# One stack of 128 quotient rows, a residual added by TensorE and copied out by ScalarE: the tail of a one-core graph attention kernel

## The chip, the cores and the metric

The kernel runs on one core of a Trainium2 chip. The metric is the device time of one execution in microseconds (us), median over runs; lower is better.

## The reference

Inputs: `x` (512 targets x 128), `adj` (512 x 512, zeros and ones, sparse), `h_neigh` (512 neighbours x 128), weights `Wq`, `Wk`, `Wv`, `Wo` (128 x 128) with biases, edge embeddings `E` (2 x 128). There are 8 heads of 16 dimensions.

```python
h = jnp.maximum(_layernorm(x, axis=-1), 0.0)
msg = h_neigh[None, :, :] + E[edge_types]          # edge_types is adj
q = (h_target @ Wq.T + bq).reshape(Bt, H, DH)      # h_target is h
k = (msg @ Wk.T + bk).reshape(Bt, Bn, H, DH)
v = (msg @ Wv.T + bv).reshape(Bt, Bn, H, DH)
scores = jnp.einsum('bhd,bnhd->bhn', q, k) / np.sqrt(DH)
scores = jnp.where(adjacency[:, None, :] == 0, -1e9, scores)
attn = jax.nn.softmax(scores, axis=-1)             # masked entries set to 0 after it
out = jnp.einsum('bhn,bnhd->bhd', attn, v).reshape(Bt, d)
return x + (out @ Wo.T + bo)
```

## The kernel before, in words

Every engine has a program of its own, written out by hand; semaphores tie them together. Each engine runs its own instructions strictly in the written order, and the order of the score tiles is the list `ORDER` (32 tiles, one per head `h` and block `t` of 128 neighbours; heads 6 and 7 are interleaved at the end, so that places 24 to 31 are the tiles of these two heads and place 31 is head 7, block 3).

**Start.** SyncE loads `x`, then the pack `pw` (the transposed `Wq` and `Wv`, and two 128x128 forms of `Wo`, 256 KB in all), then bias rows; ScalarE's queue loads `h_neigh` with `Wk`, then the adjacency in both layouts (1 MB each). VectorE computes the layer norm, TensorE turns it and projects q, k and v. For exactness q and k are split in three bf16 parts, gathered per head into `stack`. GpSimd adds `bo` to `x` early on (`resid`, line 238).

**Middle.** For each head, TensorE scores by target (lines 563 and 577), VectorE finds the masked row maximum (line 426), GpSimd splits the maximum in two bf16 parts (lines 225, 227), TensorE turns it (line 586) and ScalarE places it in the head's stack (line 323). Then TensorE scores by neighbour with the maximum already taken off (line 609), and ScalarE takes the exponential (line 351). What is not an edge is removed in one of three ways, by tile: GpSimd multiplies the exponentials by zero or one (`ON_POOL`, line 233); VectorE subtracts a veto of 2^30 from the scores on their way to the exponential (`ON_DVE`, line 446, here place 18 and places 21 to 30); or TensorE adds minus the veto in a product ahead of the scores (`ON_PE`, line 604: the rest, place 31 among them).

**Products with V.** Exponentials times `V` give 16 numerators and one denominator for each head; four heads (a "group") lie in the four 32-row quarters of a bank. Group 0 (heads 0 to 3) is accumulated in bank 5 (line 623). Group 1 (heads 4 to 7) is accumulated in two pieces, `PIECES = ((0, 3), (3, 1))`: target blocks 0 to 2 (384 columns, bank 0) and target block 3 (128 columns, bank 3), line 633.

**Tail.** `normalise(step, bank, g, first, tiles)` on VectorE (line 462) turns the 32x32 blocks of a bank (line 467), takes the reciprocal of the denominators (469), multiplies (471) and turns the quotients back into `ctxT` (476). It runs for group 0 (512 columns), for piece 0 of group 1 and for piece 1 of group 1. In `turned_U` each head keeps 32 columns of which 16 carry data, so a group fills the 128 rows of `ctxT` half, and `Wo` comes in two forms with zero rows in between, one for each group. `project_out(i, g)` on TensorE (line 639) multiplies by that form: 4 products for group 0, then 3 for piece 0 and 1 for piece 1 of group 1, accumulated in banks 4 and 5. `finish(i)` on VectorE (line 485) adds `resid` and writes `y`, SyncE stores piece 0 (192 KB, line 189) and ScalarE's queue stores piece 1 (64 KB, line 356). VectorE's order at the end is: maskings of places 21 to 30, `normalise` of group 0, of piece 0, of piece 1, `finish(0)`, `finish(1)`. Nothing follows the exponential of place 31 on ScalarE but the issue of the last store.

Of the kernel before, what the change touches and what calls it, by code (L numbers as in the profile page):

```python
# [5 lines left out]
B, N, D, H = 512, 512, 128, 8  # L6
DH = D // H
P = 128
BT, NT = B // P, N // P
# [9 lines left out]
G = 2  # L19
HG = H // G  # L20
CT = P // HG
# [13 lines left out]
PIECES = ((0, 3), (3, BT - 3))  # L35
# [3 lines left out]
TAIL_ACC, TAIL_OUT = (0, 3), (4, 5)  # L39
# [3 lines left out]
ORDER = [(h, t) for h in range(H - 2) for t in range(NT)] + [(h, t) for t in range(NT) for h in (H - 2, H - 1)]  # L43
# [2 lines left out]

LIVE_TILES = (1, 3)
ON_POOL = [(1, 1), (2, 1), (2, 3), (0, 1), (1, 3), (3, 1), (0, 3), (3, 3), (4, 1), (4, 3)]
ON_DVE = [ORDER[18]] + ORDER[21:31]
ON_PE = [tile for tile in ORDER if tile not in ON_POOL and tile not in ON_DVE]  # L50

A_BEFORE = (9, 9, 10, 12, 14, 15, 16, 17, 18, 18, 20, 21, 22, 23, 24, 26, 27, 28, 28, 30)
# [12 lines left out]
def gnn_kernel(nc, x_in, adj_b, adj_n, pack_k, pack_w, bias_rows, out):  # L65
    f32, bf16, i32 = mybir.dt.float32, mybir.dt.bfloat16, mybir.dt.int32
    ACT = mybir.ActivationFunctionType
    ALU = mybir.AluOpType
# [3 lines left out]
    with ctx:  # L72
        def sb(name, shape, dt=f32):
            return ctx.enter_context(nc.sbuf_tensor(name, shape, dt))

        def sem(name):
# [12 lines left out]
        pk = sb("pk", [P, N + D + 4])  # L89
        hnT, wkT = pk[:, 0:N], pk[:, N:N + D]  # L90
        bq_col, bk_col, e1_col = (pk[:, N + D + i:N + D + i + 1] for i in range(3))
        pw = sb("pw", [P, 4 * D])
        wqT, wvT = pw[:, 0:D], pw[:, D:2 * D]
        brow = sb("brow", [P, 2 * D])
        bv_row, bo_row = brow[:, 0:D], brow[:, D:2 * D]
        msgT = sb("msgT", [P, N])
# [11 lines left out]
        masked_scores = sb("masked_scores", [P, len(A_BANKS), N], bf16)  # L108
        masked_n = sb("masked_n", [P, len(ON_DVE), B])
        row_max = sb("row_max", [P, H, BT])  # L110
        max_parts = sb("max_parts", [P, H, MAX_ROWS, BT], bf16)
        prob = sb("prob", [P, H, NT, B])
        ident = sb("ident", [P, P])
# [8 lines left out]
        turned_U = sb("turned_U", [P, G, B // CT, CT])  # L122

        tiny_row = sb("tiny_row", [1, P], bf16)
        recip = sb("recip", [P, G, B // CT])
        ctxT = sb("ctxT", [P, G, B])
        resid = sb("resid", [P, BT, D])
        y = sb("y", [P, BT, D])
        ps = ctx.enter_context(nc.psum_tensor("ps", [P, 8, 512], f32))
# [34 lines left out]
        u_turned, recip_ready, u_scaled, ctx_ready = (  # L164
            sem("u_turned"), sem("recip_ready"), sem("u_scaled"), sem("ctx_ready"))
        tiny_zero, tiny_set = sem("tiny_zero"), sem("tiny_set")
        out_projected, resid_ready, y_ready = sem("out_projected"), sem("resid_ready"), sem("y_ready")
# [106 lines left out]
        def _(act):  # L274
# [69 lines left out]
            for k, (h, t) in enumerate(ORDER):  # L344
                if (h, t) in ON_DVE:
                    act.wait_ge(masked_ready, count_upto(ON_DVE, (h, t)))
                    scores = masked_n[:, ON_DVE.index((h, t)), :]
                else:
                    act.wait_ge(scores_n, k + 1)
                    scores = ps[:, B_BANKS[k % len(B_BANKS)], :]  # L350
                nc.scalar.activation(prob[:, h, t, :], scores, ACT.Exp, scale=DH ** -0.5).then_inc(exp_done, 1)  # L351
                for head, placed_at in PLACED_AT.items():
                    if placed_at == k:
                        place_max(head)
            act.wait_ge(y_ready, 2)
            act.dma_start(out[:, PIECES[1][0] * D:BT * D], y[:, PIECES[1][0]:BT, :]).then_inc(stored[1], 16)
            act.wait_ge(stored[1], 16)
# [2 lines left out]
        def _(dve):  # L360
# [6 lines left out]
            for t in range(BT):  # L367
                last = nc.vector.bn_stats(stats[:, t, :], xt[:, t, :])  # L368
            last.then_inc(stats_ready, 1)
            dve.wait_ge(stats_ready, 1)  # L370
            for t in range(BT):
                last = nc.vector.bn_aggr(mean_var[:, t, :], stats[:, t, :])
# [89 lines left out]
            def normalise(step, bank, g, first, tiles):  # L462

                blocks = slice(first * P // CT, (first + tiles) * P // CT)
                at = slice(first * P, (first + tiles) * P)
                dve.wait_ge(pv_done, step + 1)
                nc.vector.transpose(turned_U[:, g, blocks, :], ps[:, bank, 0:tiles * P]).then_inc(u_turned, 1)  # L467
                dve.wait_ge(u_turned, step + 1)
                nc.vector.reciprocal(recip[:, g, blocks], turned_U[:, g, blocks, DH]).then_inc(recip_ready, 1)
                dve.wait_ge(recip_ready, step + 1)  # L470
                nc.vector.tensor_tensor(
                    turned_U[:, g, blocks, 0:DH], turned_U[:, g, blocks, 0:DH],
                    recip[:, g, blocks].rearrange("p (k c) -> p k c", c=1).to_broadcast([P, tiles * P // CT, DH]),
                    ALU.mult).then_inc(u_scaled, 1)
                dve.wait_ge(u_scaled, step + 1)
                nc.vector.transpose(ctxT[:, g, at], turned_U[:, g, blocks, :].rearrange("p k c -> p (k c)")).then_inc(  # L476
                    ctx_ready, 1)

            dve.wait_ge(veto_last_ready, 1)
            dve.wait_ge(veto_odd_ready, 1)  # L480
# [1 line left out]
                mask_scores(*tile)  # L482
            normalise(0, ACC_BANK, 0, 0, BT)

            def finish(i):
                tiles = slice(PIECES[i][0], sum(PIECES[i]))
                dve.wait_ge(resid_ready, 1)
                dve.wait_ge(out_projected, 1 + i)
                nc.vector.tensor_tensor(y[:, tiles, :],  # L489
                                        ps[:, TAIL_OUT[i], :].rearrange("p (t c) -> p t c", t=BT)[:, tiles, :],  # L490
                                        resid[:, tiles, :], ALU.add).then_inc(y_ready, 1)

            normalise(1, TAIL_ACC[0], 1, *PIECES[0])
            normalise(2, TAIL_ACC[1], 1, *PIECES[1])
            finish(0)
            finish(1)

        @block.tensor
        def _(pe):

            pe.wait_ge(ones_set, 1)
            for _ in range(WARM_UP):
# [4 lines left out]
                             skip_group_check=True).then_inc(k_projected, 1)  # L507
            pe.wait_ge(idents_ready, 3)
            for i in range(HALVES):
                for t in range(HT * i, HT * (i + 1)):  # L510
                    pe.wait_ge(xn_ready, t + 1)
                    last = nc.tensor.transpose(ps[:, HT_BANKS[i], (t % HT) * P:(t % HT + 1) * P], xn[:, t, :],  # L512
                                               ident[:, :])
# [31 lines left out]
            for i in range(HALVES):  # L545
                pe.wait_ge(hT_ready[i], 1)
                nc.tensor.matmul(ps[:, Q_BANKS[i], 0:HB], wqT, hT[:, i * HB:(i + 1) * HB], start=True, stop=False,  # L547
                                 skip_group_check=True).then_inc(q_projected[i], 1)
# [87 lines left out]
                if t == V_LAST[i][-1]:  # L636
                    last.then_inc(pv_done, 1)

            def project_out(i, g):

                pe.wait_ge(ctx_ready, 1 if g == 0 else 2 + i)
                first, tiles = PIECES[i]
                for t in range(first, first + tiles):
                    last = nc.tensor.matmul(ps[:, TAIL_OUT[i], t * D:(t + 1) * D], ctxT[:, g, t * P:(t + 1) * P],  # L644
                                            pw[:, (2 + g) * D:(3 + g) * D], start=g == 0 and t == first, stop=g == G - 1,
                                            skip_group_check=True)
                if g == G - 1:
                    last.then_inc(out_projected, 1)

            for i in range(HALVES):  # L650
                pe.wait_ge(q_part_ready[i], PARTS)
# [38 lines left out]
                last_product_with_v(0, t)  # L690
            for t in V_LAST[1]:
                last_product_with_v(1, t)
            project_out(0, 0)
            project_out(1, 0)
            project_out(0, 1)
            project_out(1, 1)


# [34 lines left out]
```

## Time and profile before

| what | us |
|---|---|
| median of 3 runs | 52.49 (52.41 to 52.53) |
| the profiled execution, its own time | 52.74 |
| its span, first to last instruction | 50.6 |
| TensorE products / VectorE / ScalarE / GpSimd busy | 44.1 / 40.3 / 34.7 / 31.0 |
| mean granted clock of TensorE | 0.99 |

The times of single instructions in the rows below are in microseconds from the start of the span. The profiled execution spent 52.74 - 50.6 = 2.14 us outside its span. PE is TensorE (PEld its weight loads), DVE VectorE, ACT ScalarE, POOL GpSimd, SP SyncE.

### The profile page before, as it was taken

To read this page: it belongs to the slowest core of one execution; us is meant where nothing else is said; L and a number is where in the kernel's file an instruction comes from. 1 tells how busy PE (TensorE), PEld (TensorE's weight loads), DVE (VectorE), ACT (ScalarE), POOL (GpSimd) and SP (SyncE) were. 2 spreads that over 40 slices of the span, in tenths; PEclk is the share of its full clock that TensorE was granted. 3 is DMA by queue.
4 is the path that set the end of the run, shared out by engine and by line. 5 is a ranking of instruction groups with operands and counts; after the bars stand their busy time and mean duration, and the time that the engine had idled before them with its cause. 6 is when DMAs were issued, how large, how long until landed. Compare 5 with 4: busy or idle time off the path is not lost.

```text
span 50.6 us, 844 instructions
## 1 busy us (share of the span) xinstructions
PE 44.1 (87%) x257; PEld 17.8 (35%) x260; DVE 40.3 (80%) x115; ACT 34.7 (68%) x60; POOL 31.0 (61%) x50
## 2 busy tenths in 40 slices
PE   0899879978999679899999999999999998999800
PEld 0333215824445233234344424142222023288500
DVE  2011879598489999799999999799997999989820
ACT  0380657789996978979999898897199999400000
POOL 5790001999999999547599959990999930000000
PEclk9999999999999999999999999999999999999996
DMA  0689999960099999700000000000000000000032
GB/s 0 76 219 431 435 379 235 403 269 2 10 212 193 184 295 201 154 2 0 0 0 0 0 6 0 13 0 0 0 0 0 0 0 0 13 0 0 0 118 89
DMA packets 2070, 4.98 MB, mean 98 GB/s; under 512 B 258, under 2 KB 658, under 8 KB 1810
## 3 DMA queue, kind: packets, MB, share of 16 engines
q1 hardware_dynamic: 1490, 2.44, 21.2%
q10 hardware_dynamic: 576, 2.49, 12.7%
q8 instruction: 2, 0.03, 0.3%
q14 instruction: 2, 0.02, 0.1%
HBM read 3.08 MB, written 0.26 MB: 66 GB/s over the span
## 4 chain that ended last, share of the span: by engine, by line
PE 62%; DVE 15%; DMA 8%; ACT 5%; issue 3%; DVEq 0%
PE ps L609 15%; PE ps L577 11%; DMA xt<-x_dram 8%; PE ps L623 8%; PE ps L563 7%; PE ps L633 6%; PE ps L586 4%; PE ps L604 3%; PE ps L547 2%; PE ps L512 2%; DVE ctxT L476 2%; DVE stats L368 2%; DVE split L396 2%; DVE y L489 2%; DVE turned_U L467 2%
## 5 line engine op out<-in xcount | busy, mean ns | idle before, releaser
L426 DVE CUSTOM_DVE_ANT_0 masked_scores<-ps,mask_b 128x512 bf16<-128x512 f32 x32 | 20.1, 687 | 1.7 <-PE ps L563 1.0
L233 POOL TENSOR_TENSOR prob<-prob,live 128x512 int32<-128x512 int32 x10 | 12.6, 1275 | 0.0
L351 ACT ACTIVATE prob<-ps 128x512 f32<-128x512 f32 x21 | 11.4, 598 | 1.1 <-PE ps L609 0.8
L609 PE MATMUL ps<-stack 98*128 98x512 bf16 x32 | 10.9, 381 | 0.6 <-ACT stack L323 0.4
L577 PE MATMUL ps<-stack 96*128 96x512 bf16 x28 | 9.6, 384 | 0.2
L215 POOL TENSOR_SCALAR mask_b<-adj_b_sb 128x512 bf16<-128x512 int32 x3 | 6.3, 2111 | 4.8 <-DMA adj_b_sb<-adj_b_dram 4.8
L351 ACT ACTIVATE prob<-masked_n 128x512 f32<-128x512 f32 x11 | 6.4, 626 | 1.5 <-DVE masked_n L446 1.4
L446 DVE TENSOR_TENSOR masked_n<-ps,veto 128x512 f32<-128x512 f32 x11 | 6.8, 683 | 0.4 <-PE ps L609 0.3
L503 PE MATMUL ps<-ones 128*128 128x512 bf16 x10 | 4.2, 604 | 1.4 <-DVE ones L361 1.4
L323 ACT ACTIVATE stack<-ps 2x512 bf16<-2x512 f32 x8 | 4.7, 590 | 0.4
L609 PEld LDWEIGHTS ps<-stack 98*128 98x128 bf16 x32 | 2.8, 97 | 6.0 <-DVE masked_n L446 2.2
L623 PE MATMUL ps<-prob,V 128*32 128x512 f32 x32 | 4.3, 605 | 0.0
L577 PEld LDWEIGHTS ps<-stack 96*128 96x128 bf16 x28 | 2.5, 96 | 4.9 <-DVE row_max L426 2.7
L220 POOL TENSOR_SCALAR live<-adj_n_sb 128x512 int32<-128x512 int32 x2 | 4.1, 2048 | 0.0
L633 PE MATMUL ps<-prob,V 128*32 128x384 f32 (+1 forms) x64 | 4.0, 384 | 0.0
L225 POOL CAST max_parts<-row_max 128x4 bf16<-128x4 f32 x8 | 1.6, 203 | 3.6 <-DVE row_max L426 3.6
L563 PE MATMUL ps<-k_head,q 128*128 128x512 f32 x8 | 3.7, 605 | 0.0
L586 PE MATMUL ps<-minus,max_parts 128*2 128x128 bf16 x32 | 3.1, 218 | 0.4 <-POOL max_parts L227 0.4
L604 PE MATMUL ps<-veto,minus 128*128 128x512 bf16 x8 | 3.0, 380 | 0.0
L279 ACT ACT_TABLE_LOAD x1 | 1.3, 1283 | 2.1 <-issue 2.1
L586 PEld LDWEIGHTS ps<-minus,max_parts 128*2 128x2 bf16 x32 | 1.6, 82 | 3.3 <-POOL max_parts L227 2.7
L644 PE MATMUL ps<-pw,ctxT 128*128 128x128 f32 x16 | 2.6, 294 | 0.1
(71 smaller groups left out, 54.8 us busy)
## 6 DMA issues: line engine op xcount, KB each, us to landing
stack<-split SPq DMA_DIRECT2D x8, 192.0 KB, 4.0
adj_b_sb<-adj_b_dram ACTq DMA_DIRECT2D x1, 1024.0 KB, 7.4
adj_n_sb<-adj_n_dram ACTq DMA_DIRECT2D x1, 1024.0 KB, 10.1
pk<-pack_k_dram ACTq DMA_DIRECT2D x1, 322.0 KB, 4.4
xt<-x_dram SPq DMA_DIRECT2D x1, 256.0 KB, 4.2
pw<-pack_w_dram SPq DMA_DIRECT2D x1, 256.0 KB, 6.0
out_dram<-y SPq DMA_DIRECT2D x1, 192.0 KB, 2.0
brow<-bias_rows_dram SPq DMA_DIRECT2D x1, 128.0 KB, 9.1
```

Source lines behind the costliest of these rows:

```text
L215: nc.gpsimd.tensor_scalar(mask_b[:, t, :], adj_b_sb[:, t * N:(t + 1) * N], 0.0, MASKED, ALU.is_equal, ALU.mult).then_inc(mask_b_pool_ready, 1)
L233: nc.gpsimd.tensor_tensor(bits, bits, live[:, LIVE_TILES.index(t), :], ALU.mult).then_inc(cut_done, 1)
L323: nc.scalar.activation(stack[PAIR_ROWS:STACK, h, SIDE["q"], :], ps[PAIR_ROWS:STACK, MAX_BANK, :], ACT.Copy).then_inc(max_placed, 1)
L351: nc.scalar.activation(prob[:, h, t, :], scores, ACT.Exp, scale=DH ** -0.5).then_inc(exp_done, 1)
L426: nc.vector.tensor_tensor_reduce(out=masked_scores[:, k % len(A_BANKS), :], in0=ps[:, A_BANKS[k % len(A_BANKS)], :], in1=mask_b[:, t, :], ...
L446: nc.vector.tensor_tensor(masked_n[:, ON_DVE.index((h, t)), :], ps[:, B_BANKS[k % len(B_BANKS)], :], veto[:, t, :], ALU.subtract).then_inc ...
L563: nc.tensor.matmul(ps[:, bank, :], q32[:, t * P:(t + 1) * P], k_head_0[:, :], start=True, stop=True).then_inc(scores_b, 1)
L577: nc.tensor.matmul(ps[:, A_BANKS[k % len(A_BANKS)], :], stack[0:PAIR_ROWS, h, SIDE["q"], t * P:(t + 1) * P], stack[0:PAIR_ROWS, h, SIDE["k ...
L586: last = nc.tensor.matmul(ps[PAIR_ROWS:STACK, MAX_BANK, t * P:(t + 1) * P], max_parts[:, h, :, t], minus16[:, :], start=True, stop=True)
L609: nc.tensor.matmul(bank, stack[0:STACK, h, SIDE["k"], t * P:(t + 1) * P], stack[0:STACK, h, SIDE["q"], :], start=(h, t) not in ON_PE, stop ...
L623: last = nc.tensor.matmul(ps[j * CT:(j + 1) * CT, ACC_BANK, :], V[:, t, j, :], prob[:, j, t, :], start=False, stop=t == V_FIRST[-1], tile_ ...
L633: last = nc.tensor.matmul(ps[j * CT:(j + 1) * CT, TAIL_ACC[i], 0:tiles * P], V[:, t, HG + j, :], prob[:, HG + j, t, first * P:(first + til ...
```

## The change

1. The last tile of the order, place 31, is masked by VectorE in place of TensorE: `ON_DVE` takes one tile more, and its veto product (line 604) goes.
2. The multiplication by the reciprocals writes group 0's 16 columns of each 32-column block beside group 1's in a new tile `scaled`. One turn back for each piece (`turn_back`) gives the rows of both groups, 128 full rows, and `Wo` comes in one form: 4 products in place of 8, and `pw` has 192 KB. Group 0's own turn back goes.
3. TensorE adds `resid` with two products by the identity (`add_resid`, 384 and 128 columns, fp32), after VectorE has read bank 5.
4. ScalarE copies the two finished pieces to `y`, after its last exponential, and VectorE's two additions go.

```diff
-ON_DVE = [ORDER[18]] + ORDER[21:31]
+ON_DVE = [ORDER[18]] + ORDER[21:32]
...
-        pw = sb("pw", [P, 4 * D])
+        pw = sb("pw", [P, 3 * D])
...
+        scaled = sb("scaled", [P, B // CT, CT])
+        ctxT = sb("ctxT", [P, B])
...
+            def finish(i):
+                tiles = slice(PIECES[i][0], sum(PIECES[i]))
+                act.wait_ge(out_projected, 1 + i)
+                nc.scalar.activation(y[:, tiles, :], ps[:, TAIL_OUT[i], :].rearrange("p (t c) -> p t c", t=BT)[:, tiles, :],
+                                     ACT.Copy).then_inc(y_ready, 1)
+
+            for i in range(len(PIECES)):
+                finish(i)
             act.wait_ge(y_ready, 2)
...
                 nc.vector.tensor_tensor(
-                    turned_U[:, g, blocks, 0:DH], turned_U[:, g, blocks, 0:DH],
+                    scaled[:, blocks, g * DH:(g + 1) * DH], turned_U[:, g, blocks, 0:DH],
...
-                dve.wait_ge(u_scaled, step + 1)
-                nc.vector.transpose(ctxT[:, g, at], turned_U[:, g, blocks, :].rearrange("p k c -> p (k c)")).then_inc(
-                    ctx_ready, 1)
+            def turn_back(i):
+                first, tiles = PIECES[i]
+                dve.wait_ge(u_scaled, 2 + i)
+                nc.vector.transpose(ctxT[:, first * P:(first + tiles) * P],
+                                    scaled[:, first * P // CT:(first + tiles) * P // CT, :].rearrange(
+                                        "p k c -> p (k c)")).then_inc(ctx_ready, 1)
...
-            normalise(1, TAIL_ACC[0], 1, *PIECES[0])
-            normalise(2, TAIL_ACC[1], 1, *PIECES[1])
-            finish(0)
-            finish(1)
+            for i in range(len(PIECES)):
+                normalise(1 + i, TAIL_ACC[i], 1, *PIECES[i])
+                turn_back(i)
...
+            def add_resid(i):
+                first, tiles = PIECES[i]
+                pe.wait_ge(resid_ready, 1)
+                nc.tensor.matmul(ps[:, TAIL_OUT[i], first * D:(first + tiles) * D], ident[:, :],
+                                 resid[:, first:first + tiles, :].rearrange("p t c -> p (t c)"), start=True, stop=False,
+                                 skip_group_check=True)
+
+            def project_out(i):
+                first, tiles = PIECES[i]
+                pe.wait_ge(ctx_ready, 1 + i)
                 for t in range(first, first + tiles):
-                    last = nc.tensor.matmul(ps[:, TAIL_OUT[i], t * D:(t + 1) * D], ctxT[:, g, t * P:(t + 1) * P],
-                                            pw[:, (2 + g) * D:(3 + g) * D], start=g == 0 and t == first, stop=g == G - 1,
-                                            skip_group_check=True)
+                    last = nc.tensor.matmul(ps[:, TAIL_OUT[i], t * D:(t + 1) * D], ctxT[:, t * P:(t + 1) * P], woT,
+                                            start=False, stop=t == first + tiles - 1, skip_group_check=True)
...
-            project_out(0, 0)
-            project_out(1, 0)
-            project_out(0, 1)
-            project_out(1, 1)
+            pe.wait_ge(u_turned, 1)
+            for i in range(len(PIECES)):
+                add_resid(i)
+            for i in range(len(PIECES)):
+                project_out(i)
```

## Rows read from the trace of the kernel before

**Rows 1.** The end of the chain that ended last: start, us, what.

```profile
42.28 2.26 PE ps L633 x24
44.57 0.59 DVE turned_U L467
...
47.13 0.31 DVE ctxT L476
...
47.52 0.53 DVE y L489
...
48.09 0.29 DVE y L489
```

**Rows 2.** Timeline of VectorE: start, us, engine, line, op, tiles, count [idle before].

```profile
38.63 3.68 DVE L446 TENSOR_TENSOR masked_n<-ps,veto 128x512 f32<-128x512 f32 x6 [0.30 <-PE ps L609]
42.23 0.70 DVE L467 STREAM_TRANSPOSE turned_U<-ps 128x512 f32<-128x512 f32 x1
...
43.72 0.71 DVE L476 STREAM_TRANSPOSE ctxT<-turned_U 128x512 f32<-128x512 f32 x1
...
45.84 0.58 DVE L476 STREAM_TRANSPOSE ctxT<-turned_U 128x384 f32<-128x384 f32 x1
```

**Rows 3.** Timeline of ScalarE, the last two exponentials.

```profile
42.34 0.63 ACT L351 ACTIVATE prob<-masked_n 128x512 f32<-128x512 f32 x1
...
43.00 0.60 ACT L351 ACTIVATE prob<-ps 128x512 f32<-128x512 f32 x1
```

**Rows 4.** Timeline of TensorE and its weight loads, from place 31 on.

```profile
41.90 0.38 PE L609 MATMUL ps<-stack 98*128 98x512 bf16 x1 [0.16 <-DVE masked_n L446]
...
43.65 0.16 PEld L633 LDWEIGHTS ps<-prob,V 128*32 128x32 f32 x8 [0.63 <-ACT prob L351]
...
45.30 0.97 PEld L644 LDWEIGHTS ps<-pw,ctxT 128*128 128x128 f32 x8 [0.20 <-issue]
...
46.47 0.74 PEld L644 LDWEIGHTS ps<-pw,ctxT 128*128 128x128 f32 x6 [0.20 <-DVE ctxT L476]
...
46.91 0.50 PE L644 MATMUL ps<-pw,ctxT 128*128 128x128 f32 x3
...
47.49 0.49 PE L644 MATMUL ps<-pw,ctxT 128*128 128x128 f32 x2
```

**Rows 5.** Groups by shape: line, engine, op, tiles, count | busy us, mean ns.

```profile
L563 PE MATMUL ps<-k_head,q 128*128 128x512 f32 x8 | 3.7, 605 | 0.0
...
L633 PE MATMUL ps<-prob,V 128*32 128x384 f32 x32 | 3.1, 495 | 0.0
...
L336 ACT ACTIVATE V<-ps 128x512 f32<-128x512 f32 x1 | 0.6, 597 | 0.5 <-PE ps L534 0.5
...
L304 ACT ACTIVATE hT<-ps 128x256 f32<-128x256 f32 x2 | 0.8, 384 | 0.3
...
L318 ACT ACTIVATE warm<-eps 128x1 f32<-128x1 f32 x1 | 0.2, 203 | 0.0
```

**Rows 6.** One piece of that chain in its middle, a veto product.

```profile
19.63 0.22 PE ps L604
```

**Rows 7.** The two stores: their issue, then KB and us to landing.

```profile
48.10 0.35 SPq L189 DMA_DIRECT2D out_dram<-y  x1
48.41 0.35 ACTq L356 DMA_DIRECT2D out_dram<-y  x1
...
out_dram<-y SPq DMA_DIRECT2D x1, 192.0 KB, 2.0
out_dram<-y ACTq DMA_DIRECT2D x1, 64.0 KB, 1.8
```

**Rows 8.** The stores' transfer by stretches: A:B, us, TensorE's granted clock, DMA share, GB/s.

```profile
49.15:49.40 0.25, 1.00 1.05 393
```

**Rows 9.** The loads: TensorE's wait at the q projection, the load of pw.

```profile
8.38 0.30 PEld L547 LDWEIGHTS ps<-hT,pw 128*128 128x128 f32 x2 [0.21 <-issue]
...
pw<-pack_w_dram SPq DMA_DIRECT2D x1, 256.0 KB, 6.0
```

More of the change, by code:

```diff
@@ L91, in gnn_kernel @@
         bq_col, bk_col, e1_col = (pk[:, N + D + i:N + D + i + 1] for i in range(3))
-        pw = sb("pw", [P, 4 * D])
-        wqT, wvT = pw[:, 0:D], pw[:, D:2 * D]
+        pw = sb("pw", [P, 3 * D])
+        wqT, wvT, woT = pw[:, 0:D], pw[:, D:2 * D], pw[:, 2 * D:3 * D]
         brow = sb("brow", [P, 2 * D])
@@ L125, in gnn_kernel @@
         recip = sb("recip", [P, G, B // CT])
-        ctxT = sb("ctxT", [P, G, B])
+        scaled = sb("scaled", [P, B // CT, CT])
+        ctxT = sb("ctxT", [P, B])
         resid = sb("resid", [P, BT, D])
@@ L464, in normalise @@
                 blocks = slice(first * P // CT, (first + tiles) * P // CT)
-                at = slice(first * P, (first + tiles) * P)
                 dve.wait_ge(pv_done, step + 1)
@@ L483, in _ @@
             normalise(0, ACC_BANK, 0, 0, BT)
[L485 to L491, printed above, removed]
-            normalise(1, TAIL_ACC[0], 1, *PIECES[0])
-            normalise(2, TAIL_ACC[1], 1, *PIECES[1])
-            finish(0)
-            finish(1)
+            for i in range(len(PIECES)):
+                normalise(1 + i, TAIL_ACC[i], 1, *PIECES[i])
+                turn_back(i)
         @block.tensor
@@ L637, in last_product_with_v @@
                     last.then_inc(pv_done, 1)
-            def project_out(i, g):
-                pe.wait_ge(ctx_ready, 1 if g == 0 else 2 + i)
+            def add_resid(i):
                 first, tiles = PIECES[i]
-                for t in range(first, first + tiles):
-                    last = nc.tensor.matmul(ps[:, TAIL_OUT[i], t * D:(t + 1) * D], ctxT[:, g, t * P:(t + 1) * P],
-                                            pw[:, (2 + g) * D:(3 + g) * D], start=g == 0 and t == first, stop=g == G - 1,
-                                            skip_group_check=True)
-                if g == G - 1:
-                    last.then_inc(out_projected, 1)
+                pe.wait_ge(resid_ready, 1)
[5 more added lines that the diff above has]
+                pe.wait_ge(ctx_ready, 1 + i)
+                for t in range(first, first + tiles):
+                    last = nc.tensor.matmul(ps[:, TAIL_OUT[i], t * D:(t + 1) * D], ctxT[:, t * P:(t + 1) * P], woT,
+                                            start=False, stop=t == first + tiles - 1, skip_group_check=True)
+                last.then_inc(out_projected, 1)
             for i in range(HALVES):
@@ L712, in by_dim @@
         return w.reshape(H, DH, -1).transpose(1, 0, 2).reshape(D, -1)
-    wo = np.zeros((G, HG, CT, D), Wo.dtype)
-    wo[:, :, :DH] = Wo.T.reshape(G, HG, DH, D)
+    wo = Wo.T.reshape(G, HG, DH, D).transpose(1, 0, 2, 3).reshape(P, D)
     cols = [by_dim(bq), by_dim(bk), E[1][:, None], np.zeros((D, 1), E.dtype)]
@@ L722 @@
         "pack_k_dram": np.concatenate([hn.T, by_dim(Wk).T, *cols], axis=1),
-        "pack_w_dram": np.concatenate([by_dim(Wq).T, Wv.T, *wo.reshape(G, P, D)], axis=1),
+        "pack_w_dram": np.concatenate([by_dim(Wq).T, Wv.T, wo], axis=1),
         "bias_rows_dram": np.concatenate([bv, bo])[None],
```

## The prediction, made before the changed kernel ran

> **What bounds the kernel now.** I read the chain that ended last first, from its end backwards, because everything the change touches lies in the last 9 us. It ends in VectorE: turn, reciprocal, product and turn back of piece 0, the same four for piece 1 until 47.44, then the addition of piece 0 and, right behind it on the same engine, that of piece 1, over at 48.38 [rows 1]. Only then is the second store issued, at 48.41, and it lands 1.8 us later, at 50.2; the first, issued at 48.10, lands at 50.1 [rows 7]. Ahead of 44.57 the chain names TensorE's products with V [rows 1]. The timelines correct that: the last eight of piece 0 had their weights loaded at 43.65, after a wait of 0.63 us for ScalarE [rows 4], whose exponential of place 31 ran from 43.00 to 43.60 [rows 3]. It could not start before, since the exponential of place 30 ended at 42.97, and that one had started at 42.34 behind VectorE's masking of place 30: six maskings in 3.68 us, 0.68 each, so started 0.60 apart, the last from 41.63 to 42.31 [rows 2]. So the path to the end is: masking of place 30 on VectorE, two exponentials, products with V, VectorE's eight steps, two additions, the store.
>
> **The veto of place 31.** Its product on TensorE goes, worth 0.22 us there [rows 6], so the scores that began at 41.90 and took 0.38 [rows 4] begin at about 41.68 and are there at 42.06. VectorE's new masking is next after place 30's. By the spacing it starts at 42.23 (where the turn of group 0 starts now) and ends at 42.91; the scores are there 0.17 us before. The exponential follows a masking by 0.03 us (42.31 to 42.34 [rows 2, 3]): 42.94, and as one that reads `masked_n` it takes 0.63 in place of 0.60, until 43.57 against 43.60. Gain 0.03. The bounds: if the masking starts only when place 30's has ended (42.34), the exponential runs from 43.05 to 43.68, a loss of 0.08; better than 0.03 it can hardly be, as the masking is bound by the one before. I take 0.03, the spacing of the five pairs in [rows 2]. TensorE's own 0.22 is worth nothing: it waits for ScalarE at 43.65 anyway.
>
> **Group 0's steps on VectorE** start 0.60 later, at 42.83. They lose the turn back of 0.71 us; what is left took from 42.23 to 43.72 (1.49 us) [rows 2] and now ends at 44.32. Piece 0's first turn can start at 44.54, so 0.22 us cover it. The removed turn back ended at 44.43 before 44.57, and so was hidden: no gain from it. If VectorE were late by more than that, each further part would come straight off the end.
>
> **VectorE's eight steps for group 1** keep their shapes (the turn back of piece 0 has 128x384 before and after, 0.58 us [rows 2]); only the target of the product moves. I cost this at nothing. Their last ends at 47.44 - 0.03 = 47.41.
>
> **TensorE between 45.27 and the first turn back.** Before, group 0's four products (8 instructions, loads for 0.97 us from 45.30 [rows 4]) filled this gap, and piece 0's weights were loaded at 46.47, behind the turn back that ended at 46.42. Now two products by the identity stand there, 512 fp32 columns in all. Head 0's eight instructions of 512 columns were busy for 3.7 us together [rows 5] and make up four products of that width, so 512 columns cost 0.93 us: done at 46.20. The first turn back is there at 46.39: cover 0.19. The lower bound of the effect is nothing. The upper bound takes durations without overlap, 2 x 0.495 for 384 columns [rows 5] and 0.49 for the pair of 128 [rows 4], 1.48 us: done at 46.75, late by 0.36. I take the first, since it is the same kind of product, back to back on the same engine. The new wait for VectorE's turn of group 0 (over at 42.83 + 0.70 = 43.53) holds up nothing at 45.27, and `resid` was made long before.
>
> **Three products, then one.** The work behind each turn back is the same: piece 0's ends at 47.41 now [rows 4], 47.38 then; piece 1's load starts 0.05 after the turn back, 47.46, and the product takes 0.49 [rows 4]: 47.95.
>
> **The additions go, ScalarE's copies come.** ScalarE has been idle since 43.60, and behind its two new waits for TensorE only the second store's issue is queued; SyncE waits for copy 0 as it did for the addition. Copies from the accumulation banks took 0.597 us for 512 columns and 0.384 for 256 [rows 5]; straight between and beyond, 384 columns take 0.49 and 128 take 0.28. Copy 0: 47.41 to 47.90, SyncE's store issued at 47.92 against 48.10. Copy 1 waits for TensorE (47.95 + 0.03 = 47.98) and no longer for the engine: 47.98 to 48.26, the store issued at 48.29 against 48.41. Before, 47.44 to the last y took 0.94 us; now it takes 0.85. Bounds: as long as the next larger shape (0.597 and 0.384), copy 1 runs from 48.04 to 48.42, a loss of 0.04 at the issue; as short as the nearest smaller (0.384 and 0.203), a gain of 0.20. I take the straight line, since two points of the same engine give it.
>
> The rule table of the Trainium skill's page "ScalarE: Activation LUTs" (Rules for kernel authors) says to give `add` and its like to VectorE, up to about three times faster per element in bf16. Here, fp32 from the banks, VectorE's own last steps took 0.53 and 0.29 us [rows 1], no less than the line for ScalarE gives. By the page's formula for an ACTIVATE (186 ns + 0.833 ns per column) an estimate for the copies is 0.506 and 0.293 us, and the sum would be 0.015 us longer.
>
> **The loads.** `pw` shrinks from 256 to 192 KB. It is the second load on SyncE's queue and landed 6.0 us after its issue, and TensorE's q projection at 8.38 waited for no transfer [rows 9]. No gain; 64 KB less traffic beside the adjacency could only help steps that don't bind. If a load did come later by a few hundredths, it would show there.
>
> **Sum.** Second store issued 0.03 + 0.09 = 0.12 us earlier; the profiled execution would have taken 52.74 - 0.12 = 52.62. That execution was 0.25 above the median of the runs shown, so I put the same difference on the median: 52.49 - 0.12 = 52.37. A measurement of this kernel can tell about 0.2% (0.1 us) from no change, so this forecast lies just beyond that.
>
> **Rivals.**
> *A, the stores share their way (chance 0.10).* In 49.15 to 49.40 the 16 DMA engines were fully busy with both stores [rows 8]. If the bytes' end is set by when the bulk begins, the first store counts, which is issued 0.18 earlier: 52.31. Against it: the second store is the last to land, and its issue moved only 0.12. The Trainium skill's page "Trainium Kernel Development and Optimization" (Key Constraints) says that transfers from the SP and ACT queues run on the same 16 engines and interleave; by that rule the first one's start counts too, and the sum would be this rival's.
> *B, the gain is eaten (0.23).* If the masking of place 31 starts at 42.34, the tail is 0.08 late and the copies give 0.09 back: 52.48. If ScalarE's copies are as long as the larger shapes, the store is issued 0.04 later than before: 52.53. For it: 0.03 us decide in the hand-over between two engines. Against: the five equal spacings.
> *C, slower: the identity products come too late (0.10).* They stand on TensorE right in front of the products that the first turn back releases. The point from which it decides is 46.39. Done at 46.75, they put the end of piece 0's products at 47.74 and piece 1's right behind, so that ScalarE's copies follow each other: 47.77 to 48.26 and 48.29 to 48.57. The store is issued at 48.60, 0.19 later than before: 52.68. For it: fp32, 512 columns, and nothing left out. Against: the measured spacing.
> *D, the change does not free what it says (0.05).* If VectorE, with one masking more, is not ready at 44.54 (group 0's steps longer than the 1.71 us from 42.83), piece 0 starts late by the rest; with 0.2 us over, 52.57.
>
> **The numbers.** Forecast 0.52, A 0.10, B 0.23, C 0.10, D 0.05. The forecast's and A's spread lies around the bound of 0.1 us: I count 0.47 of their 0.62 as faster by over 0.2%. Within 0.2%: their other 0.15, 0.20 of B and 0.03 of D, together 0.38. Slower: C with 0.10 and the far ends of B (0.03) and D (0.02), 0.15. The range goes from 52.25 (A with copies at their short bound) to 52.60, which leaves C out.
>
> **What would show it.** The exponential of place 31 reads `masked_n`, starts near 42.94 and is over by 43.60. VectorE is idle for about 0.2 us before the turn of piece 0 (44.54). TensorE's loads of the identity end by 46.2, with a wait for the turn back at 46.4 behind them. ScalarE shows copies of 0.49 and 0.28 us, the second waiting for TensorE; the stores are issued near 47.9 and 48.3. I am wrong if TensorE is still adding the residual when the turn back ends, if the chain goes through both copies, or if the last store is issued earlier and the end does not move.

## The result, and the profile after

The changed kernel takes 52.09 us, median of 20 runs (51.74 to 52.68), against 52.53 us for the kernel before (20 runs beside it, 52.04 to 52.98). The ratio is 0.9925, 95% interval 0.9902 to 0.9948. The ratios here leave out the executions that took over 1.5% longer than the fastest of the same kernel (three of these 20), while medians and mean spans take in all. The forecast was 52.37 with a range from 52.25 to 52.60: the right sign, but the gain is 0.44 us where 0.12 was forecast.

The profiled execution of the changed kernel took 51.80 us with a span of 49.8 us. Its chain that ended last, from the last group of maskings on (start, us, what):

```profile
35.18 0.70 DVE masked_n L458
...
37.18 5.74 ACT prob L354 x10
42.91 0.04 issue
42.96 0.90 PE ps L640 x8
43.85 0.02 issue
43.88 0.59 DVE turned_U L478
...
45.15 0.58 DVE ctxT L491
...
46.44 0.32 DVE ctxT L491
46.76 0.04 issue
46.80 0.50 PE ps L658 x2
47.30 0.02 issue
47.33 0.28 ACT y L362
```

Beside [rows 1]: the two additions at the end of VectorE are gone; behind the last turn back (46.75) there is TensorE's one product and ScalarE's short copy. Every step also begins some 0.7 us earlier than it did, long before the code that was changed. The timelines of VectorE, ScalarE, TensorE with its loads, and the issues of the stores:

```profile
35.18 2.48 DVE L458 TENSOR_TENSOR masked_n<-ps,veto 128x512 f32<-128x512 f32 x4
37.96 4.28 DVE L458 TENSOR_TENSOR masked_n<-ps,veto 128x512 f32<-128x512 f32 x7 [0.30 <-PE ps L616]
42.16 0.71 DVE L478 STREAM_TRANSPOSE turned_U<-ps 128x512 f32<-128x512 f32 x1
...
43.88 0.58 DVE L478 STREAM_TRANSPOSE turned_U<-ps 128x384 f32<-128x384 f32 x1 [0.27 <-PE ps L640]
...
37.18 5.73 ACT L354 ACTIVATE prob<-masked_n 128x512 f32<-128x512 f32 x10
46.76 0.84 ACT L362 ACTIVATE y<-ps 128x384 f32<-128x384 f32 x2 [3.85 <-PE ps L658]
47.63 0.35 ACTq L368 DMA_DIRECT2D out_dram<-y  x1
...
44.61 1.13 PE L650 MATMUL ps<-resid,ident 128*128 128x384 f32 x4
...
45.78 0.74 PEld L658 LDWEIGHTS ps<-pw,ctxT 128*128 128x128 f32 x6 [0.23 <-DVE ctxT L491]
...
47.27 0.35 SPq L192 DMA_DIRECT2D out_dram<-y  x1
```

What to see. Seven maskings in 4.28 us keep the spacing of 0.60 (six in 3.68 [rows 2]). VectorE is idle for 0.27 us before the turn of piece 0. The identity products lie between 44.61 and 45.74, and the load for piece 0's projection follows the turn back (45.73) by 0.05, as before (46.42 to 46.47 [rows 4]).

ScalarE's copies by shape (line, engine, op, tiles, count | busy us, mean ns | idle before) have the forecast's lengths:

```profile
L362 ACT ACTIVATE y<-ps 128x384 f32<-128x384 f32 x1 | 0.5, 491 | 3.9 <-PE ps L658 3.9
...
L362 ACT ACTIVATE y<-ps 128x128 f32<-128x128 f32 x1 | 0.3, 278 | 0.1
```

To take the start out of the comparison I measure from the start of the last four maskings in a row (`masked_n` x4; 35.85 before, 35.18 here) to the issue of the second store (48.41 [rows 7], 47.63 here): 12.56 us before, 12.45 in the changed kernel. In all later traces with the same tail this stretch came out within 0.01 us of the same value, while its start lay anywhere from 35.18 to 36.03 us (without the runs that hold a load back). So a tail's price can be read from one trace, and a start's only from many executions. To the issue of the first store the stretch is 12.25 us before and 12.09 after; that this one counts too is shown further down.

### The profile page after: what moved, and what is told of

It is laid out like the page before. It is cut to its first block and busy times, and to the rows that moved or that the text cites. A ratio compares the mean times of both kernels' runs of the same rounds, so it can differ in the third digit from the quotient of the medians.

```text
span 49.8 us, 833 instructions
## 1 busy us (share of the span) xinstructions
PE 44.0 (88%) x253; PEld 17.7 (35%) x255; DVE 39.4 (79%) x113; ACT 35.3 (71%) x62; POOL 30.7 (62%) x50
## 3 DMA queue, kind: packets, MB, share of 16 engines
q10 hardware_dynamic: 576, 2.49, 13.1%
## 5 line engine op out<-in xcount | busy, mean ns | idle before, releaser
L354 ACT ACTIVATE prob<-ps 128x512 f32<-128x512 f32 x20 | 10.8, 598 | 1.0 <-PE ps L616 0.8
L354 ACT ACTIVATE prob<-masked_n 128x512 f32<-128x512 f32 x12 | 7.0, 628 | 1.5 <-DVE masked_n L458 1.4
L458 DVE TENSOR_TENSOR masked_n<-ps,veto 128x512 f32<-128x512 f32 x12 | 7.4, 683 | 0.4 <-PE ps L616 0.3
L362 ACT ACTIVATE y<-ps 128x384 f32<-128x384 f32 (+1 forms) x2 | 0.8, 384 | 3.9 <-PE ps L658 3.9
```

Source lines behind the costliest of these rows:

```text
L458: nc.vector.tensor_tensor(masked_n[:, ON_DVE.index((h, t)), :], ps[:, B_BANKS[k % len(B_BANKS)], :], veto[:, t, :], ALU.subtract).then_inc ...
```

## The experiments

Theory T: the whole gain lies in the tail. Theory L: the part over 0.12 us comes from the loads, because `pw` has 64 KB less. Theory N: the start only varies by chance. All times are set against runs of the kernel before on the same chip.

**1. The changed kernel again** (no edit).

> The changed kernel once more, on the chip of this set, as the measure for the others. Both theories: a ratio near 0.9925, some 0.4 us faster than the kernel before. Of that my sum gives the tail 0.12 us; theory L (loads) gives the other 0.27 us to the load of x, which lands earlier because pw has 64 KB less; theory T (tail) has all of it behind 42 us.

Measured: 52.04 us against 52.57, ratio 0.9882 (0.9842 to 0.9922, 6 runs). The tail's stretch is 12.45, the time from the second store's issue to the end of the span 2.15 (2.23 and 2.20 in two traces of the kernel before), and outside the span 2.02 (2.10).

The end follows the first store's issue more closely than the second's. In all twenty traces it comes 2.49 to 2.54 us after the first. After the second it comes 2.19 to 2.23 us later where the two are issued 0.30 or 0.31 apart (eleven traces), and 2.14 to 2.16 where they are 0.36 or 0.37 apart (nine).

**2. The changed kernel with `pw` at 256 KB.**

```diff
-        pw = sb("pw", [P, 3 * D])
+        pw = sb("pw", [P, 4 * D])
...
-np.concatenate([by_dim(Wq).T, Wv.T, wo], axis=1)
+np.concatenate([by_dim(Wq).T, Wv.T, wo, np.zeros((P, D), Wo.dtype)], axis=1)
```

> The changed kernel with pw padded to 256 KB again (64 KB of zeros nobody reads). Theory L: about 0.27 us of the gain goes, ratio near 0.998, and x lands about 0.3 us later than in the changed kernel (median over executions; a single trace can differ by as much). Theory T: ratio stays at 0.9925. Theory N (x's landing varies between executions and has nothing to do with pw): ratio stays too.

Measured: 52.32 us, ratio 0.9945 (0.9912 to 0.9977). That is nearer to T's and N's 0.9925 than to L's 0.998, but the changed kernel beside it had 0.9882, and against that the gain shrinks, which neither T nor N explains. But x had landed 3.8 us after its issue in its trace, no later than in run 1. What that trace shows late is another thing, the k projection. TensorE's rows of run 2 (two loads of the warm-up, the k projection, x's turn; then its stretch from 6 to 7 us with busy time, granted clock 1.00, DMA share and GB/s), and then those of run 1:

```profile
3.98 0.15 PEld L510 LDWEIGHTS ps<-ones 128*128 128x128 bf16 x1 [0.28 <-issue]
4.41 0.15 PEld L510 LDWEIGHTS ps<-ones 128*128 128x128 bf16 x1 [0.28 <-issue]
...
5.68 1.85 PE L513 MATMUL ps<-msgT,pk 128*128 128x512 f32 x2
...
7.37 0.66 PE L519 MATMUL ps<-ident,xn 128*128 128x128 f32 x4
...
6.00:7.00 1.00, 1.00 (x2) 1.00 1.06 428
```

```profile
5.51 1.12 PE L513 MATMUL ps<-msgT,pk 128*128 128x512 f32 x2 [0.33 <-ACT msgT L285]
6.95 1.00 PE L519 MATMUL ps<-ident,xn 128*128 128x128 f32 x4 [0.32 <-DVE xn L391]
...
6.00:7.00 1.00, 0.68 (x3) 1.00 1.04 397
```

The same two instructions took 1.85 us in one execution and 1.12 in the other. The warm-up products ahead of them were started 0.43 us apart for 512 bf16 columns, which is the 1.2 GHz level; the 512 bf16 columns of a veto product later took 0.22 [rows 6], 2.4 GHz. In run 2 the k projection still ran at the lower level, in run 1 at the upper one. The view's granted clock reads 1.00 in the stretch from 6 to 7 us in both, because it counts the time ahead of the trace's first clock record as 1.00. That first record is the rise to 2.4 GHz itself: 7.30 us after the start of the span in run 2, 4.32 in run 1. Over the twenty traces it lies between 4.13 and 7.35 us.

**3. The kernel before with `pw` at 192 KB and the last 64 KB later.**

```diff
-            sp.dma_start(pw[:, :], pack_w).then_inc(pw_loaded, 16)
+            sp.dma_start(pw[:, 0:3 * D], pack_w).then_inc(pw_loaded, 16)
...
+            sp.wait_ge(x_loaded, 16)
+            sp.dma_start(pw[:, 3 * D:4 * D], pack_wo).then_inc(wo_loaded, 16)
...
+            pe.wait_ge(wo_loaded, 16)
             project_out(0, 0)
```

> The kernel before, with pw loaded as 192 KB at its place and the last 64 KB (group 1's form of Wo) in a load of its own on SyncE's queue once x is in. Theory L: ratio near 0.995 (0.27 us faster) with the tail unchanged. Theories T and N: 1.000.

Measured: 52.28 us, ratio 0.9932 (0.9900 to 0.9964), with the tail's stretch at 12.56 as before. T falls as the whole explanation: a version without any of the tail's changes gains 0.27 us. But this trace too spent 2.02 us outside the span, not 2.10, so part of it is no matter of loads. (The last line of the edit, one wait more on TensorE, is also in runs 5, 6 and 10, which load a part of `pw` by itself.)

**4. The changed kernel with place 31's veto on TensorE.**

```diff
-ON_DVE = [ORDER[18]] + ORDER[21:32]
+ON_DVE = [ORDER[18]] + ORDER[21:31]
```

> The changed kernel with place 31's veto back on TensorE. By my sum the exponential of place 31 ends 0.03 us later: ratio 0.9925 + 0.0006, not to be told apart in the time, but the trace shows it starting 0.66 us after that of place 30 rather than 0.60. If the masking on VectorE costs or gives more than that, the time moves by over 0.1 us.

Measured: 52.18 us, ratio 0.9912 (0.9875 to 0.9949), not to be told from the changed kernel. The stretch is 12.47 against 12.45, and the exponential of place 31 starts 0.66 us after that of place 30, as expected: part 1 is worth 0.02 us where the prediction had 0.03.

**5 to 7. Smaller and larger `pw`.** Run 5 is the kernel before with 128 KB in `pw` and both forms of Wo later; run 6 the changed kernel with Wo later; run 7 the changed kernel with `pw` padded to 512 KB.

```diff
+            sp.dma_start(pw[:, 0:2 * D], pack_w).then_inc(pw_loaded, 16)
...
+            sp.wait_ge(x_loaded, 16)
+            sp.dma_start(pw[:, 2 * D:4 * D], pack_wo).then_inc(wo_loaded, 16)
```

(In run 6 the later load is `pw[:, 2 * D:3 * D]`; in run 7 the edit is that of run 2 with five blocks of zeros.)

> The kernel before with pw cut to 128 KB (Wq and Wv) and both forms of Wo (128 KB) loaded later, on SyncE's queue once x is in; the tail as before. Theory L (bytes issued early beside x and the k pack cost time): twice the step of the 192 KB run, 0.3 to 0.55 us faster than before, ratio 0.990 to 0.994. Theory N (spread of executions): 1.000 within 0.003.

> The changed kernel with Wo (64 KB) taken out of pw and loaded later in the same way. Theory L: another 0.1 to 0.3 us faster than the changed kernel, ratio 0.985 to 0.990. Theory N: as the changed kernel, 0.991 to 0.9925.

> The changed kernel with pw padded to 512 KB by zeros nobody reads (320 KB more, still early enough for TensorE's q projection if the engines keep 430 GB/s). Theory L with a price per byte (0.3 us for 64 KB): over 1 us slower than the changed kernel. Theory L with a price by sharing of the 16 engines (64 KB at 430 GB/s is 0.15 us): 0.4 to 0.75 us slower than the changed kernel. Theory N: as the changed kernel.

Measured: run 5 52.29 us, ratio 0.9956 (0.9929 to 0.9983); run 6 52.12, 0.9937 (0.9895 to 0.9979); run 7 52.31, 0.9958 (0.9925 to 0.9991). Neither form of L's price holds: 128 KB bring no more than 192, and 512 KB cost no more than 256. N's 1.000 within 0.003 for run 5 is met only if the share outside the span, 0.08 us or 0.0015, is taken off. What remains of L is a step between 192 and 256 KB.

**8. VectorE copies in place of ScalarE.**

```diff
+            def finish(i):
+                tiles = slice(PIECES[i][0], sum(PIECES[i]))
+                dve.wait_ge(out_projected, 1 + i)
+                nc.vector.tensor_copy(y[:, tiles, :],
+                                      ps[:, TAIL_OUT[i], :].rearrange("p (t c) -> p t c", t=BT)[:, tiles, :]
+                                      ).then_inc(y_ready, 1)
```

(behind both `turn_back`s on VectorE; ScalarE's `finish` is left out.)

> The changed kernel with VectorE in place of ScalarE copying the two pieces out. One look, read from the start of the last maskings (the first VectorE masking of the group of four) to the issue of the second store, which was 12.56 us before and 12.45 us in the changed kernel. A copy by VectorE of 384 columns from the banks starts when TensorE's three products end (about as now) and takes 0.53 to 0.56 us: the second copy takes 0.29, so 12.46 to 12.50 if VectorE is as good, since it is free by then. So nearly all of the tail's gain is the order of work (first piece finished before the second product ends), not the engine; theory S (ScalarE's shorter copy carries the gain): 12.56.

Its timeline at the end:

```profile
47.18 0.86 DVE L500 COPY y<-ps 128x384 f32<-128x384 f32 x2
47.22 0.30 PEld L660 LDWEIGHTS ps<-pw,ctxT 128*128 128x128 f32 x2 [0.27 <-DVE ctxT L483]
47.77 0.36 SPq L192 DMA_DIRECT2D out_dram<-y  x1
48.07 0.35 ACTq L360 DMA_DIRECT2D out_dram<-y  x1
```

The stretch is 12.47, where ScalarE's copies give 12.45: theory S falls, ScalarE itself is worth 0.02 at the issue of the second store. At the end of the span it is worth more: from the start of the same maskings to the end run 8 takes 14.66 us, the nine traces with ScalarE's copies 14.58 to 14.62, the kernel before 14.77 to 14.79. The first copy is the longer one by 0.07 on VectorE (0.558 against 0.491), so the first store is issued 12.17 us into the stretch in place of 12.09. Of the tail's 0.11 us at the second store's issue, 0.02 come from place 31 (run 4) and 0.02 from ScalarE, so 0.07 are left for what run 8 has in common with the changed kernel. They lie in front of the first copy: before, the addition began at 47.52, 0.08 behind the last turn back (47.44, [rows 1]); VectorE's copy began at 47.18, 0.01 behind it (46.86 + 0.31). The addition waited for two semaphores, `resid_ready` and `out_projected`, the copy for one; that this makes the 0.07 is argued, not tested.

**9, 17, 18. `pw` held back until x is in** (kernel before, one line).

```diff
+            sp.wait_ge(x_loaded, 16)
             sp.dma_start(pw[:, :], pack_w).then_inc(pw_loaded, 16)
```

> The kernel before, with the issue of pw (256 KB, unchanged) held on SyncE until x has landed; the bias rows and ones queue behind it. Theory L-share (pw's rows delay x's on the shared DMA engines): x lands well before the 3.7 to 4.2 us after its issue seen so far, 3.2 to 3.6; the time falls by 0.2 us or more unless pw itself then comes too late for the q projection (pw would land near 8, needed at 7.9 to 8.4), in which case the trace shows TensorE waiting for pw. Theory N (x's landing is not pw's doing): x lands at 3.7 to 4.2 as before, and the time rises by pw's lateness or stays.

> The kernel before with pw held until x has landed, second look. If pw's bytes beside x's are what delays x: first use of x at 4.35 to 4.55 us. If not: 4.6 to 5.0 as in the traces with pw at 256 KB.

> The same kernel, third look; the same expectation: 4.35 to 4.55 us if pw beside x is the cause, 4.6 to 5.0 if not.

Measured in run 9: 55.89 us, median of six (54.51 to 58.36); the ratio 1.0422 (1.0328 to 1.0516) is that of the two shortest alone. Runs 17 and 18 are one execution each, 55.40 and 55.73 us. `pw` comes too late, as TensorE's load at the q projection shows in run 9.

```profile
4.69 0.88 DVE L369 BATCH_NORM_STATS2 stats<-xt 128x6 f32<-128x128 f32 x4 [1.83 <-DMA xt<-x_dram]
...
10.58 1.35 PEld L548 LDWEIGHTS ps<-hT,pw 128*128 128x128 f32 x4 [2.26 <-DMA pw<-pack_w_dram]
```

For x it is the first row that counts. With nothing of `pw` in flight, x's first use began at 4.69, 4.55 and 4.61 us in the three traces. It did not come earlier than with `pw` at 192 KB beside it (4.34 to 4.66), and x landed 3.8 to 3.9 us after its issue, not 3.2 to 3.6. Three traces are few against the spread, but they give no support to plain sharing of the DMA engines between `pw` and x.

**10. The same 256 KB as two loads with rows of 1 KB** (kernel before).

```diff
-            sp.dma_start(pw[:, :], pack_w).then_inc(pw_loaded, 16)
+            sp.dma_start(pw[:, 0:2 * D], pack_w).then_inc(pw_loaded, 16)
+            sp.dma_start(pw[:, 2 * D:4 * D], pack_wo).then_inc(wo_loaded, 16)
```

> The kernel before, with pw's 256 KB issued at the same place as two loads of 128 KB (rows of 1 KB each in place of rows of 2 KB). Theory L-rows (what counts is the size of pw's rows next to x's last rows; 1 and 1.5 KB are alike, 2 and 4 KB are alike in the runs so far): about 0.25 us faster than before, ratio 0.995. Theory L-bytes (what counts is the bytes queued right behind x): 1.000 within 0.002. Theory N: 1.000.

Measured: 52.27 us, ratio 0.9961 (0.9924 to 0.9997). That is 0.2 us, of which 0.08 lie outside the span (2.02 again). The mean span is 50.32 us (+-0.15) against 50.45 (+-0.04): too close to tell rows from bytes. With the 0.08 us taken off, theory N's 1.000 is within the interval too.

**11. The kernel before again** (no edit).

> The kernel before once more, one look, for where x lands and how long the k projection takes. Theory L: x lands 3.9 us or more after its issue. Theory N: anywhere from 3.6 to 4.2. The stretch from the start of the last four maskings to the second store's issue is 12.56 us whatever the start.

Measured: 52.31 us (one execution), x landed 3.6 us after its issue, as early as in any trace, with `pw` at 256 KB; stretch 12.57; outside the span 2.13. L in its strict form (x always late beside 256 KB) falls.

**12. Nine warm-up products in the changed kernel.**

```diff
-WARM_UP = 10
+WARM_UP = 9
```

> The changed kernel with 9 warm-up products in place of 10 (they fill a scratch bank and nothing reads them). In the changed kernel's traces the k projection starts at 5.69 us, when the warm-up ends, although its input was ready at 5.3 to 5.4. If that queue caps what an earlier x and k pack bring, 9 products let it start at 5.3 to 5.5 and the kernel is 0.1 to 0.3 us faster than the changed one, ratio 0.987 to 0.990. If the shorter warm-up makes TensorE's clock rise later, the k projection takes 1.8 us more often and the gain is lost or turned: ratio 0.992 or more.

Measured: 52.08 us, ratio 0.9934 (0.9896 to 0.9973), as the changed kernel. In its trace the k projection began at 5.63, later than the end of the warm-up, since x and the k pack were late in that execution. No gain that can be told.

**13. One wait more on TensorE in the kernel before.**

```diff
+            pe.wait_ge(pw_loaded, 16)
             project_out(0, 0)
```

> The kernel before with one wait more on TensorE ahead of the projection (for pw, long in), nothing else. The stretch to the second store and the start stay. Theory O (the time outside the span depends on the program's make-up, such as an engine's number of instructions, not on what the change computes): outside the span 2.02 us in place of 2.10 is possible; theory O' (it comes with the loads' make-up: another input, or other rows of pw): 2.10. Time over all executions: 0 or 0.09 us less.

Measured: 52.35 us, ratio 0.9956 (0.9920 to 0.9993). The stretch is 12.56, the mean span 50.35 (+-0.15) as before, and the time outside the span is 2.03 us (+-0.02, 12 executions) against 2.105 (+-0.006, 116 executions of the kernel before). A wait for a semaphore that was raised 38 us earlier makes the kernel 0.08 us faster. Theory O stands, O' falls: neither loads nor arithmetic are needed for it. Not every wait does it: run 9, with one wait more on SyncE, spent 2.11 us outside the span (+-0.03, 6 executions). Every program here whose TensorE part differs from that of the kernel before spent 2.00 to 2.04 us outside the span on average, run 14 among them, which only loses one product there; the programs with the same TensorE part spent 2.10 to 2.13. What it is in TensorE's part that decides was not tested.

**14. Part 1 alone, in the kernel before.**

```diff
-ON_DVE = [ORDER[18]] + ORDER[21:31]
+ON_DVE = [ORDER[18]] + ORDER[21:32]
```

> The kernel before with place 31's veto on VectorE alone (part 1 of the change by itself). VectorE then has group 0's turn back still in its queue: by my durations it is free at 42.83 + 2.20 = 45.03 where piece 0 is there at 44.54, so 0.4 to 0.5 us are lost at the end (stretch 12.56 becomes 12.95 to 13.1), which shows that part 1 pays only together with part 2. Theory O: outside the span 2.02 is possible; O': 2.10.

Its VectorE rows, from the turn of group 0:

```profile
42.53 0.70 DVE L467 STREAM_TRANSPOSE turned_U<-ps 128x512 f32<-128x512 f32 x1
...
44.01 0.71 DVE L476 STREAM_TRANSPOSE ctxT<-turned_U 128x512 f32<-128x512 f32 x1
...
44.65 0.54 DVE L467 STREAM_TRANSPOSE turned_U<-ps 128x384 f32<-128x384 f32 x1
```

Measured: 52.73 us, ratio 1.0021 (0.9981 to 1.0062); the stretch is 12.90, 0.34 longer than before, a little under the 0.4 to 0.5 expected. The turn of piece 0 now follows the turn back of group 0 without a gap. Moving the masking needs the removed turn back: with it, it gains 0.02 (run 4); without it, it costs 0.34.

**15 and 16. The changed kernel with 192 KB and with 256 KB once more.**

> The changed kernel again (pw 192 KB). Mean span 50.05 to 50.15 us if the start's gain is real, outside the span 2.02.

> The changed kernel with pw padded to 256 KB again. If the start's 0.15 us come with pw's size: mean span 50.25 to 50.35 us, 0.15 to 0.2 above the changed kernel beside it, as in the first pair of samples (50.33 against 50.09). If that was chance: within 0.05 of it.

Measured: 52.17 us, ratio 0.9918 (0.9886 to 0.9950), and 52.41 us, ratio 0.9947 (0.9910 to 0.9983). Mean spans 50.13 (+-0.11) and 50.38 (+-0.17): the first as expected, the second 0.03 above its range, and the two 0.26 apart, as L has it.

**The start, over all executions.** Each execution left its span, so the starts can be compared although their traces are few.

| kernel | executions | mean span, us | outside the span, us |
|---|---|---|---|
| before | 116 | 50.45 +- 0.04 | 2.105 |
| before, `pw` small or in rows of 1 KB (runs 3, 5, 10) | 36 | 50.28 +- 0.07 | 2.03 |
| changed | 38 | 50.10 +- 0.07 | 2.03 |
| changed, `pw` 256 KB (runs 2, 16) | 24 | 50.36 +- 0.10 | 2.02 |
| before, one wait more on TensorE (run 13) | 12 | 50.35 +- 0.15 | 2.03 |
| changed, other edits, `pw` at most 192 KB (runs 4, 6, 12) | 36 | 50.16 +- 0.09 | 2.03 |
| changed, `pw` 512 KB (run 7) | 12 | 50.27 +- 0.12 | 2.03 |

In the changed kernel 64 KB of `pw` are worth 0.26 us of the span (+-0.12), and 0.20 (+-0.09) if runs 4, 6, 7 and 12 are counted in. In the kernel before it is 0.17 (+-0.08), but the runs with the smaller loads also have the wait of run 13, and against that run alone the difference is 0.07 (+-0.16), so there it isn't shown. The traces agree: x's first use begins at 4.50 us on average in the ten traces with `pw` at 192 KB or less or in 1 KB rows (4.34 to 4.66), and at 4.75 in the seven with 256 KB or more (4.37 to 4.99). And what begins early ends early: the last four maskings start either 30.93 us after x's first use, or 28.45 us after the end of the k projection, whichever is later. In run 1, 4.52 + 30.93 = 35.45 was measured to the hundredth, in run 2, 5.68 + 1.85 + 28.45 = 35.98. Of the 17 traces without a held `pw`, 13 lie within 0.02 us of this and the other four within 0.12.

Which of the two is later depends on TensorE's clock. Where it rose before 5.3 us, the k projection took 1.12 or 1.13 us and x bound the start. In the four traces where it rose at 7.25 us or later (runs 2, 3, 4 and 10), the k projection took 1.80 to 1.89 us and bound it, and an earlier x was worth nothing. An estimate from the 17 traces: each with its own k projection where the clock rose after 5.6 us, and x's first use at 4.50 in place of 4.75, gives 0.18 us on average. So x's 0.25 us is enough for the gain, and the clock lets some of it through and not all.

That the size of `pw` matters in the changed kernel is shown; by what way it reaches x is not, since 128 KB bring no more, 512 KB cost no more, and holding `pw` back brought nothing. The padding of runs 2, 7 and 16 also lengthens `pw` in the core's own memory and its rows in the load, and no run tells these apart from the bytes.

## Why the prediction was wrong

**The tail was right up to the second store's issue.** Forecast 0.12 us there, measured 0.11 (12.56 to 12.45). Its steps: place 31's masking gained 0.02 where 0.03 was forecast (run 4); VectorE had 0.27 us to spare before piece 0 where 0.22 was forecast; the identity products were out of the way in time, though their records end at 45.74, level with the end of the turn back (45.73), and not 0.19 before it, since they took 1.13 us where 0.93 was forecast; the copies took 0.491 and 0.278 us, as forecast, the second waiting for TensorE; from the last turn back to the store's issue 0.88 us against 0.97, the forecast 0.09. Rival C did not come: the load for piece 0's products still follows its turn back by 0.05. It was close, the whole cover of 0.19 had gone. Rivals B and D did not come either. Rival A did, though it was given a chance of 0.10.

**"Second store issued 0.12 us earlier; the profiled execution would have taken 52.74 - 0.12."** This is the step that failed: the sum took the gain at the second store's issue as the gain of the kernel, and put at nothing what lies behind that issue, outside the span and at the start. Three terms were missing:

- *Behind the issue, 0.06 us.* From the second store's issue to the end of the span it took 2.23 and 2.20 us before, 2.15 in both first traces of the changed kernel. The first store is issued 0.36 before the second now, where it was 0.31. Run 8, with the stores 0.30 apart, took 2.19. From the first store's issue it is 2.49 to 2.54 us in every trace, and that issue came 0.16 us earlier (12.25 to 12.09). The smaller store, issued last, ends with the larger one. That is rival A's mechanism and nearly its size (52.31, so 0.06 more). It agrees with what the Trainium skill's page "Trainium Kernel Development and Optimization" (Key Constraints) says, that both queues' transfers interleave on the same engines.
- *Outside the span, 0.08 us.* The 2.14 us outside the span (2.10 with the trace's unrounded span of 50.64) were taken as fixed, and are 2.105 in the kernel before on average and 2.03 in the changed one. Run 13 got the same from one idle wait.
- *"The loads. No gain", some 0.2 us.* The span fell by 0.35 on average; without the tail's 0.11 and the 0.06, 0.18 are left for the start. Padding `pw` back took 0.26 +- 0.12, and the estimate from x's first use is 0.18. I had asked only whether TensorE waited for `pw`, and it did not [rows 9]. The transfer that binds the start in most traces is x, which the chain of the kernel before had in it (0.73 to 4.90 us), and I did not ask whether its landing would stay.

Together 0.11 + 0.06 + 0.08 + 0.18 = 0.43 us, and the means of all executions, 52.56 and 52.13, differ by 0.43. This is no proof, as the 0.18 are what was left over. The range failed with the sum: it was made from the bounds of the tail's prices alone, while the 116 executions of the kernel before already lie anywhere from 52.06 to 53.18 us.

TensorE's clock did not carry the gain, as far as the executions show. The k projection took 1.8 us or more in runs 2, 3, 4 and 10, with large and small `pw`, and 1.45 or less in all other traces but run 9's (1.73). Of the 17 traces without a held `pw`, the five whose mean granted clock reads 0.99 all had the rise between 4.71 and 5.27 us; I take it that other executions with such a reading are like them. Executions with a reading below 1.00 are about as frequent before (43 of 116), in the changed kernel with `pw` at most 192 KB (30 of 74) and with more (16 of 36). And among these alone the mean spans are 50.35 (+-0.06), 50.01 (+-0.05) and 50.25 (+-0.11), so the differences stay.

The Trainium skill's page "ScalarE: Activation LUTs" (Rules for kernel authors) gives `add` and its like to VectorE, as up to about three times faster per element in bf16. No run here has these steps in bf16. In fp32 out of the banks ScalarE's copies took 0.491 and 0.278 us and VectorE's 0.558 and 0.291 (run 8), so here ScalarE is the faster one, by little.

## What to carry to other kernels

Where executions spread, find the stretch that repeats to 0.01 us between two fixed instructions and read a tail's change from that; for what lies in front of it, collect spans. When an edit changes a load, don't ask only who waits for that load, but whether the other loads on the chain still land when they did. When two stores share the end, price the larger one's issue too, and not only the last one's. And don't build on gains of under 0.1 us in a kernel of this length without looking at the time outside the span, which an idle wait can move.

## What the runs showed of the hardware that was not expected

- The time outside the span is steady for a program and differs between programs that do the same: 2.105 us (116 executions) against 2.03 with one idle wait more on TensorE (run 13), and 2.11 with one more on SyncE (run 9). What in the program decides is open.
- Products of the same shape took 1.85 and 1.12 us at the same place in two executions, because TensorE's clock rose at 7.30 us in one and at 4.32 in the other. TensorE had been busy since 1.44 us in both, and the view's granted clock read 1.00 for both.
- The end of the span comes 2.49 to 2.54 us after the issue of the first and larger store (192 KB) in all twenty traces, whether the second (64 KB) is issued 0.30 or 0.37 us behind it.
- x's landing varied from 3.6 to 4.2 us after its issue for one and the same program (kernel before, two traces).
